# Newton-Schulz iteration: the next X and its transposed by products of one go, against turning X in each iteration

## The reference

```python
X = X / (jnp.sqrt(jnp.sum(X * X, axis=(1, 2), keepdims=True)) + 1e-07)
for a, b, c in NS_COEFFS:          # five
    A = X @ X.transpose(0, 2, 1)
    B = b * A + c * (A @ A)
    X = a * X + B @ X
```

## Time and profile before

| | before |
|---|---|
| median of 3 runs | 765.18 us |
| the profiled execution | 764.44 us |
| its span, first to last instruction | 762.5 us |
| mean granted TensorE clock | 0.970 |
| TensorE busy | 662.8 us, 87% |
| weight loads busy | 549.6 us, 72% |
| VectorE busy | 545.3 us, 72% |
| ScalarE busy | 408.4 us, 54% |
| GpSimd busy | 235.5 us, 31% |
| chain of waits, by engine | PE 52%, DVE 28%, ACT 7%, issue 7%, POOL 3%, DMA 2% |
| chain, largest lines | PE CC L828 16%, PE YB L828 12%, PE HB L828 10% |

### The profile page before, as it was taken

The page is one execution under the profiler, slowest core; times in us unless marked ns, Lnnn a source line. Parts: engine busy times, 40 slices in busy tenths (PEclk is TensorE's granted clock), DMA queues, the critical chain, the costliest instruction groups (busy, mean ns, idle before and its releaser), DMA issues.

```text
span 762.5 us, 22396 instructions
## 1 busy us (share of the span) xinstructions
PE 662.8 (87%) x8887; PEld 549.6 (72%) x8887; DVE 545.3 (72%) x1893; ACT 408.4 (54%) x1061; POOL 235.5 (31%) x299
## 2 busy tenths in 40 slices
PE   4788787999998889999999999999999999996865
PEld 2667565777786677878788788877878778784654
DVE  6865887685564496777868778687777867758673
ACT  3576352543543547656465564755657476462541
POOL 2422122146762131312213131132221313117761
PEclk9799989999999899999999999999999999999997
DMA  8300000041102024453552545444454544101221
GB/s 276 123 2 2 1 3 1 2 174 38 46 20 78 30 63 141 135 181 120 155 180 93 182 129 172 154 140 161 130 178 140 159 135 142 36 5 32 61 80 52
DMA packets 40152, 75.38 MB, mean 99 GB/s; under 512 B 9712, under 2 KB 24432, under 8 KB 40048
## 3 DMA queue, kind: packets, MB, share of 16 engines
q1 hardware_dynamic: 36224, 68.08, 28.0%
q0 software_dynamic: 2048, 4.33, 1.9%
q10 hardware_dynamic: 1776, 1.54, 0.6%
HBM read 64.73 MB, written 9.20 MB: 97 GB/s over the span
## 4 chain that ended last, share of the span: by engine, by line
PE 52%; DVE 28%; ACT 7%; issue 7%; POOL 3%; DMA 2%; SPq 0%; DVEq 0%; ACTq 0%; POOLq 0%
PE CC L828 16%; PE YB L828 12%; PE HB L828 10%; PE M L828 8%; DVE hb L1698 4%; DVE Am L1408 2%; POOL xsrc L447 2%; ACT hb L562 2%; DVE Mp L1414 2%; PE CC L921 1%; ACT XT L562 1%; DVE comb L1517 1%; PE M L1010 1%; PE CC L960 1%; POOL r L422 1%
## 5 line engine op out<-in xcount | busy, mean ns | idle before, releaser
L422 POOL TENSOR_TENSOR r<-r,half 128x3 f32<-128x3 f32 (+1 forms) x78 | 88.6, 1142 | 206.8 <-DVE r L1285 112.9
L1408 DVE TENSOR_TENSOR Am<-CC,shifts 128x192 f32<-128x192 f32 x150 | 47.6, 352 | 80.9 <-PE CC L828 80.7
L562 ACT ACTIVATE XT<-CC 128x256 f32<-128x256 f32 x150 | 50.9, 382 | 85.0 <-PE CC L922 84.6
L828 PE MATMUL YB<-e_s,hb 128*128 128x128 f32 x560 | 78.3, 283 | 5.9 <-DVE hb L1698 5.9
L562 ACT ACTIVATE hb<-HB 128x512 f32<-128x512 f32 x86 | 51.3, 597 | 54.6 <-PE HB L828 53.4
L828 PE MATMUL HB<-xsT,e_s 128*128 128x128 f32 x560 | 78.8, 284 | 1.7 <-issue 1.7
L828 PEld LDWEIGHTS YB<-e_s,hb 128*128 128x128 f32 x560 | 68.6, 191 | 16.1 <-DVE hb L1698 9.5
L1698 DVE TENSOR_TENSOR hb<-hb,cwb 128x512 f32<-128x512 f32 x70 | 76.1, 1087 | 0.0
L828 PEld LDWEIGHTS HB<-xsT,e_s 128*128 128x128 f32 x560 | 68.3, 192 | 4.6 <-issue 1.8
L828 PE MATMUL CC<-X,Mp 64*64 64x64 f32 x1800 | 57.0, 234 | 16.5 <-DVE Mp L1414 16.5
L828 PE MATMUL CC<-Am 64*64 64x64 f32 x1800 | 55.9, 233 | 14.0 <-DVE Am L1408 13.9
(11 more groups left out here) (229 smaller groups left out, 1505.9 us busy)
## 6 DMA issues: line engine op xcount, KB each, us to landing
e_s<-in_e1T SPq DMA_DIRECT2D x35, 512.0 KB, 4.6
e_s<-in_e2T SPq DMA_DIRECT2D x35, 512.0 KB, 5.6
cwb<-tile_weights SPq DMA_DIRECT2D x35, 512.0 KB, 3.7
sorted_rows<-e_s SPq DMA_DIRECT2D x5, 476.0 KB, 10.2
xs<-sorted_rows SPq DMA_DIRECT2D x35, 68.0 KB, 5.3
sorted_out<-yo SPq DMA_DIRECT2D x35, 64.0 KB, 2.9
out<-xnT_all SPq DMA_DIRECT2D x8, 256.0 KB, 2.1
x_all<-in_x SPq DMA_DIRECT2D x1, 1408.0 KB, 14.8
```

The source lines that it names most:

```text
L422: return pool.tensor_tensor(dst, src, expo[:, 0:n], ALU.pow)
L562: return nc.scalar.activation(out_, in_, func, **kw)
L828: return pe.matmul(out_, lhsT, rhs, start=start, stop=stop)
L1408: nc.vector.tensor_tensor(Am[g][:, :, :], PROD[g], shifts[:, it, :].unsqueeze(1).to_broadcast([P, 3, HD]), ALU.add)\
```

## The change

Newton-Schulz iterations 0 to 3 compute X and its transposed in the apply: 12 products per group where there were 6. The transposed comes from the same operands with their roles exchanged (Mp is symmetric). One ScalarE copy of 128x384 takes both to SBUF. The next gram reads the transposed from there, so that turns and XT copies stay in iteration 0 only. The halves and columns of the products from iteration 1 on are placed anew, and the buffer yT, used at the end of the kernel, shares the memory of an expert-weight buffer to make room.

```diff
-        X = [sb(f"X{g}", [P, 3, HD]) for g in range(G)]
+        XX = [sb(f"XX{g}", [P, 2, 3 * HD]) for g in range(G)]
+        X = [XX[g][:, :, :].rearrange("p b c -> p (b c)")[:, HD:4 * HD].rearrange("p (w c) -> p w c", w=3) for g in range(G)]
+        TURNED = [[XX[g][:, :, :].rearrange("p b c -> p (b c)")[:, n * HD:(n + 1) * HD] for n in (0, 4, 5)] for g in range(G)]
...
-        yT = sb("yT", [P, 2, P])
+        yT = e1_s[RING - 1][:, 0:2, :]
...
+        BOTH = [CC[g][:, :].rearrange("p (b c) -> p b c", b=2)[:, :, 0:3 * HD] for g in range(G)]
+        SQUARED = [CC[g][:, 2 * P:8 * P].rearrange("p (w c) -> p w c", w=3)[:, :, 0:HD] for g in range(G)]
...
+        PAIRS = (("X", 0, low), ("X", 0, high), ("X", 2, low), ("X", 2, high), ("X", 1, low), ("X", 1, high),
+                 ("T", 1, low), ("T", 1, high), ("T", 0, low), ("T", 0, high), ("T", 2, low), ("T", 2, high))
+        PLACE = {("X", 0): HD, ("X", 1): 2 * HD, ("X", 2): 4 * P, ("T", 0): 0, ("T", 1): 4 * P + HD, ("T", 2): 4 * P + 2 * HD}
...
             def xt(i, g, it):
-                act.wait_ge(e_t[g], NI * i + it + 1)
+                act.wait_ge(e_t[g], i + 1)
...
             def ns_x(i, g, it):
...
-                a(X[g][:, :, :], PROD[g], ACT.Copy).then_inc(e_x[g], 1)
+                if it < NI - 1:
+                    a(XX[g][:, :, :], BOTH[g], ACT.Copy).then_inc(e_x[g], 1)
+                else:
+                    a(X[g][:, :, :], PROD[g], ACT.Copy).then_inc(e_x[g], 1)
...
-                    if st % 4 == 0:
+                    if st == 0:
                         for g in range(G):
                             xt(i, g, st // 4)
...
-                xt_in[g].wait()
-                for w, c in GRAM:
-                    rows, n = (high, 1) if w == 2 else (low, w)
-                    half = other(c) if w == 2 else c
-                    ins = mm(ns_out(g, w, half), XT[g][rows, n, c], XT[g][rows, n, c])
+                if it:
+                    x_turn[g].wait(skip=1 if it == NI - 1 else 0)
+                    for w, c in SQUARE:
+                        half = other(c) if w == 2 else c
+                        ins = mm(ns_out(g, w, half), TURNED[g][w][c], TURNED[g][w][c])
+                else:
+                    xt_in[g].wait()
+                    for w, c in GRAM:
+                        rows, n = (high, 1) if w == 2 else (low, w)
+                        half = other(c) if w == 2 else c
+                        ins = mm(ns_out(g, w, half), XT[g][rows, n, c], XT[g][rows, n, c])
...
                 for w, c in SQUARE:
-                    half = other(c) if w == 2 else c
-                    ins = mm(ns_out(g, w, c), Am[g][half, w, :], Am[g][half, w, :])
+                    half = other(c) if w == 2 or w == 1 and it else c
+                    ins = mm(ns_out(g, w + 1 if it else w, c), Am[g][half, w, :], Am[g][half, w, :])
...
-                for w, c in APPLY:
-                    half = other(c) if w == 2 and it < NI - 1 else c
-                    ins = mm(ns_out(g, w, half), Mp[g][c, w, :], X[g][c, w, :])
+                if it == NI - 1:
+                    for w, c in APPLY:
+                        ins = mm(ns_out(g, w, c), Mp[g][c, w, :], X[g][c, w, :])
+                else:
+                    for what, w, c in PAIRS:
+                        at = PLACE[what, w]
+                        if what == "X":
+                            half = other(c) if w == 2 else c
+                            ins = mm(CC[g][half, at:at + HD], Mp[g][c, w, :], X[g][c, w, :])
+                        else:
+                            half = other(c) if w else c
+                            ins = mm(CC[g][half, at:at + HD], X[g][c, w, :], Mp[g][c, w, :])
...
                         if st % 4 == 0:
-                            ns_turn(g, st // 4 == NI - 1)
+                            if st == 0:
+                                ns_turn(g)
...
-                nc.vector.scalar_tensor_tensor(Mp[g][:, :, :], PROD[g], NS[it][2],
+                nc.vector.scalar_tensor_tensor(Mp[g][:, :, :], SQUARED[g] if it else PROD[g], NS[it][2],
```

More of the change, by code:

```diff
@@ L917, in sums, with ns_turn @@
                 mm(CB[g][:, 0:3], bdones[:, :], r3[g][:, 0, :]).then_inc(e_ssb[g], 1)
-            def ns_turn(g, last_step):
-                x_turn[g].wait(skip=1 if last_step else 0)
+            def ns_turn(g):
+                x_turn[g].wait()
                 pe.transpose(CA[g][0:HD, 0:P], X[g][:, 0, :], ident[:, :])
@@ L925, in ns_gram, with ns_square @@
             def ns_gram(g, it):
-                xt_in[g].wait()
-                for w, c in GRAM:
-                    rows, n = (high, 1) if w == 2 else (low, w)
-                    half = other(c) if w == 2 else c
-                    ins = mm(ns_out(g, w, half), XT[g][rows, n, c], XT[g][rows, n, c])
+                if it:
[9 more added lines that the diff above has]
+                        ins = mm(ns_out(g, w, half), XT[g][rows, n, c], XT[g][rows, n, c])
                 ins.then_inc(e_prod[g], 1)
-            def ns_square(g):
+            def ns_square(g, it):
                 am_in[g].wait()
                 for w, c in SQUARE:
-                    half = other(c) if w == 2 else c
-                    ins = mm(ns_out(g, w, c), Am[g][half, w, :], Am[g][half, w, :])
+                    half = other(c) if w == 2 or w == 1 and it else c
+                    ins = mm(ns_out(g, w + 1 if it else w, c), Am[g][half, w, :], Am[g][half, w, :])
                 ins.then_inc(e_prod[g], 1)
@@ L1182, in body @@
                         elif st % 4 == 2:
-                            ns_square(g)
+                            ns_square(g, st // 4)
                         else:
```

## The result

The changed kernel takes 746.07 us (median of 4 runs, 745.61 to 748.52) where the kernel before takes 765.12 (4 runs): ratio 0.9753, 95% interval 0.9725 to 0.9782. The prediction was 755.3 us in a range of 749.5 to 766.0. The profiled execution of the changed kernel is the slowest of its four (748.52 us).

What follows compares the result with a forecast made beforehand. TensorE's order of work was taken as the bound. Eleven steps at -0.83 us (-9.1) and steps 0, 1, 2 and 14 at -0.2 each (-0.8) made -9.9: 765.2 to 755.3 us, range 749.5 to 766.

Steps and rivals of the forecast that it cites:

- The price of the products: Each doubled apply, 48 records, would take 0.84 us to the next work, 0.23 more, set by the fullest quadrant.
- the rival by the record: Each doubled apply costs 1.22 us, in proportion to its records: +0.70 us a step, 776 us in all; chance 0.12.
- The copy: ScalarE's joint copy of X and its transposed, 128x384, would take about 490 ns, bounds 382 and 597.
- The four places: The stretches from apply to next gram in each step: -0.53, -0.35, -0.20 and +0.25 us, together -0.83 a step.
- the loss at the fourth: Last apply-to-gram stretch: turned probabilities come later and copy prT begins 0.25 us later, a loss of 0.25 us a step.
- In iteration 2 TensorE itself is the bound: In steady steps VectorE waits for the gram except in iteration 2, where TensorE bounds; 11 steps at -0.83 us, -9.1.
- Steps 0 to 2 and 14 at -0.2 each: Steps 0, 1, 2 and 14 were expected between 0 and -0.83 us each, taken as -0.2, in all -0.8 us.
- The clock: Only in steps 0, 1, 2 and 14: added products cost more in stretches at 1.2 GHz, within the -0.2 us each.
- No added wait, yT, gram and square at no cost: Gram and square from iteration 1 on keep their quadrant fill, and yT's new buffer adds no wait: 0 us.
- absorbed in the first place: Rival: VectorE's Mp of iteration 1 comes no earlier, losing the 0.53 us; -0.30 a step, 761 us; chance 0.14.
- a copy costs two: Rival: a copy over two banks costs two copies, 0.67 us; -0.47 us a step, 759 us; chance 0.08.
- nothing measurable: Rival: several of the other rivals meet and the kernel stays at 765 us; chance 0.04.

Runs made afterwards that it cites:

- the second trace: Profiled execution of a repeat of the changed kernel, nothing edited; the repeat measured 746.47 us against 766.45 for the kernel before, ratio 0.9738.
- the kernel before with the square earlier: Kernel before with the square of the next q and k one stage earlier on ScalarE, ahead of iteration 2's XT copies: 759.47 us against 766.45, ratio 0.9907.
- the kernel with the early turn: Changed kernel with probabilities turned ahead of iteration 3's apply and prT copied before X: first 771.68 us against 798.47 (kernel before, slower chip), again 736.77, ratio 0.9613.

## Why the prediction was right in the steps and wrong in the sum

- **The price of the products: right.** 0.86 us for the doubled apply (0.84 said), and in its sharpest form: 1.55 us for the same records on two quadrants. The choice of the near end by the quadrants' fill in the earlier trace rows stands; the rival by the record, given 0.12, is refuted.
- **The copy: right** (491 ns).
- **The four places: right** to 0.07 us, with the loss at the fourth. They gave -0.87 us and the whole step -0.92; -0.83 was said. In steps 5 to 13 the forecast gives 7.5 us and 8.3 came.
- **"In iteration 2 TensorE itself is the bound": wrong outside the steady steps.** I read it off step 8, where 1.1 us of expert products hide how late Am is, and carried it to steps 3 and 4 with the same -0.83. There nothing hides it. The missing part is 1.1 us in each of steps 2 to 4 and 0.6 in step 14, some 3.9 us together from gram to square. This is the step that failed, and the term that it left at nothing is enough to bring the time below the range: 746.07 + 3.9 is 750.0 us (an estimate; other parts of steps 3 and 14 gave some of it back, so that step 3 fell by 1.6 us and step 14 not at all). What I should have followed is the second effect of a removed instruction: the copy to XT cost ScalarE not only its 382 ns but a wait of 1.7 us, with ready work behind it. The text said of ScalarE only that it has room.
- **Steps 0 to 2 and 14 at -0.2 each: too small.** Step 0 gave 1.7 us in the second trace. Two parts of it gain, 1.0 us and 1.65, and the rest of the step loses 1.0. The 1.0 is around place 3, where the turn stood on TensorE, waiting for a late copy, ahead of work that was ready; it is the same mistake on another engine. The 1.65 is from the apply of iteration 1 to the square of iteration 2, where the kernel before had 3.4 us at a granted clock of 0.50 and the changed one had 1.00, so that it is partly the clock. Step 1 gave 0.2 and step 14 lost 0.3, so the caution was right for two of the four.
- **The clock: not in the sum.** Of the 5.1 us that step 4 is shorter in the second trace, about 3 go with two stretches at 1.2 GHz that the kernel before had there and the changed one had not. I had the clock only as a cost to the products in stretches at 1.2 GHz, and no term for stretches that come or go. It can't be called shown that the change is the cause of the missing ones: the first trace of the changed kernel had one of them still, and the kernel before with the square earlier had lost one too. At about the same mean clock the two kernels are still 17 to 18 us apart, so the forecast of 9.9 would have failed without the clock as well.
- **No added wait, yT, gram and square at no cost: right**; gram to square and square to apply of iterations 3 and 4 are unchanged to 0.02 us.
- **The rivals** "absorbed in the first place", "a copy costs two" and "nothing measurable" did not occur.

In numbers, the 18.9 us of span between the kernel before and the second trace of the changed one: 8.3 in steps 5 to 13 (7.5 said), 6.7 in steps 3 and 4 (1.7 said), 2.3 in step 2 (0.2), 1.7 in step 0 (0.2), 0.2 in step 1 (0.2), -0.3 in step 14 (0.2), nothing at the end. That the second trace's surplus is so near the median's is partly luck: 3 us of it are the clock in step 4, and the first trace had only a part of that; its span is 15.8 us below that of the kernel before. The range failed because its low end was built from a better fourth place alone, and not from the steps that I hadn't read stage by stage.

## To carry to other kernels

When an instruction goes, count what waited behind its wait, on its own engine, in each kind of step: here a copy of 0.38 us that waited 1.7 us held the ready work behind it for that long. A steady step is a poor guide to the others, since its cover hides late work; read one step of each kind. And these small products cost by the fullest quadrant of the array, so that spreading them over four quadrants made twice the products cost 40% more (0.61 to 0.86 us).

## What the runs showed of the hardware

- 48 records of 64x64 take 0.86 us on four quadrants, 1.55 on two; 24 take 0.61 at 8 on the fullest, 0.84 at 12. The page "TensorEngine Tiling (Array Packing)" of the Trainium skill, section "Key Properties", says that tiles operate independently; these runs agree. Its "Gotcha 1: PSUM Pressure" says that different row tiles can't access one bank at the same time; here low-to-low and high-to-high wrote the same bank, in different partitions, at two records per 58 ns ((1.55 - 0.86) / 12 on the fullest quadrant). In the trace of the changed kernel four records, one for each quadrant, start 7 ns apart (417.453, 417.460, 417.467 and 417.473 us), and the next four begin 59 ns after the first.
- Chips differ: on two of the four chips of the experiments, the kernel before took 797.7 and 798.5 us in place of 766. The steady steps had the same period there to 0.01 us. Nearly all of the time lay in the steps in which rows are scattered and gathered by indirect DMAs (with the same kernel on both kinds of chip, step 3 takes 64.5 and 66.3 us in place of 50.0 and 51.6, step 14 61.7 and 61.5 in place of 47.2 and 46.4) and, for 3 to 5 us, after them. Engines sit there for up to 7.5 us with no releaser of the core's own, as here (VectorE, from the first run of the kernel with the early turn):

```profile
196.10 0.36 DVE L1444 SCALAR_TENSOR_TENSOR Mp<-CC,rests 128x192 f32<-128x192 f32 x1 [3.28 <-remote]
```

What holds them there stays open.
